# A cross-attention block followed by a recurrent block: head norm, softmax division and score issue rearranged, in a new order of work

## Chip, core and metric

One core of one Trainium2 chip runs the whole program. The metric is the device time of one execution in microseconds. Engines named here: PE is TensorE (PEld its weight loads), DVE is VectorE, ACT is ScalarE, POOL is GpSimd, SP is SyncE, whose queue issues nearly all DMAs.

## The reference

Eight batches, each of 128 channels by 256 positions, pass two layers. All of it is float32. Cut to what matters:

```
# layer 0: attention, 16 heads of 8 channels, 256 positions
q, kv = LN(x + pos), LN(ctx + pos)          # over the 128 channels
S = (q Wq)(kv Wk)^T / sqrt(8)               # per head, 256 x 256
y = softmax(S) (kv Wv);  r = y Wo + q
x1 = r + W2 gelu(W1 LN(r) + b1) + b2
# layer 1: recurrence, 128 tokens, 256 features = 32 heads of 8
xn = LN(x1); sx = shift(xn) - xn            # five mixes of xn and sx
r, k, v, gate, w = projections of the mixes
s_t = k_t v_t + w_t s_(t-1)                 # 8 x 8 state per head
out = r_t (u k_t v_t + s_(t-1))
att = head_norm(out) * gn_w + gn_b          # mean and variance over 8 features
x2 = x1 + (att * gate) Wo
out = x2 + sigmoid(xr Fr) * (relu(xk Fk)^2 Fv)
```

## The kernel before

**Stages.** A batch goes through four stages. Stage a (L373 to L399, and `top`): the two layer norms, projections q, k, v, and the split of q and k into three bf16 parts whose products give float32-like scores. The parts are written to DRAM (`spill`, L303) and read back stacked by head (`stack`, L309, 48 rows per head, even heads at partitions 0 to 47, odd heads at 64 to 111). `top` (PE L401, DVE L789) computes all scores with queries on partitions only to find each query's maximum; `guard` feeds the negated maxima back by DMA as two more rows. Stage h: `scores` again with keys on partitions (L422), `probs` as ACT exponentials (L609), `sums` (L437) as products with padded values whose extra columns of ones give the softmax denominators, `ctxn` the division, `wo`, a layer norm and the feed-forward (`h_centre` to `x1`). Stage r: layer norm, five mixes (`maa1` to `mixed`), projections `vg` and `rk` (16 instructions each), the decay, `values` and `v_rep` (values through DRAM and back, replicated), `kv` on POOL, two `scan` instructions on DVE. Stage o: `bonus`, `read`, head norm, gate, output projection, second layer norm, feed-forward and store.

**Order.** Nothing is scheduled at run time. The table `AT` gives every step an offset, `PERIOD` a distance between batches; `due` and `ticks` walk the sum, and each engine's instructions are issued in that order (L101 to L111). Only the order within an engine matters; waits are semaphores. In a full period the engines hold stage a of one batch, h of the batch ahead of it, r of the next ahead, and o of the one before that.

**Scores.** Heads alternate between two banks, `a_even` and `a_odd` (or `h_even`, `h_odd`). The PE issues head n once the consumer is through with head n-2, so it may write one bank while the other is read.

**Division.** `h_sum` has channels and denominators interleaved on partitions, queries along the free axis. DVE shuffles the denominators to the channels, takes a reciprocal of 128x256 elements and multiplies, twice (L801 to L810).

**Readout and head norm.** `read` uses the scanned state as weights and a 128x16 head indicator as the moving operand, 16 products per half, 32 instructions in a batch for both; the output has tokens on partitions. DVE adds the bonus, takes mean and variance over each head's 8 features in six steps (`heads`, L895), POOL the power -0.5 (`hrs`), DVE multiplies (`attn`), the PE turns it back (`turn_att`), ACT applies the affine (`ag`), DVE the gate (`agg`). `own` (PE L524, ACT L683) turns the values to tokens for this.

Of the kernel before, what the change touches and what calls it, by code (L numbers as in the profile page):

```python
# [9 lines left out]
ALU = mybir.AluOpType  # L10
ACT = mybir.ActivationFunctionType
AX = mybir.AxisListType
# [30 lines left out]
           ("FkT", 2 * E), ("FrT", 2 * E), ("FvT", 2 * E), ("heads", 16), ("Wo", 2 * C),  # L43
# [3 lines left out]
for _n, _w in WEIGHTS:  # L47
# [6 lines left out]
PERIOD = 729  # L54
# [3 lines left out]
        "load": 0, "spill": (1534, 1599, 1724), "stack": 1900, "guard": 1914, "values": 3359, "v_rep": (3409, 3436), "store": 4813,  # L58
    },
    "PE": {  # L60
        "centre": 1199, "var": 1234, "spread": 1293, "qk": 1350, "v": 1487,
        "top": (1627, 1638, 1663, 1672, 1690, 1705, 1739, 1740, 1762, 1811, 1825, 1834, 1846, 1864, 1878, 1887), "guard": 1919,
        "scores": (2108, 2123, 2265, 2278, 2311, 2338, 2341, 2350, 2399, 2405, 2428, 2495, 2549, 2561, 2587, 2598), "sums": (2354, 2370, 2571, 2623),
        "wo": 2731, "h_centre": 2743, "h_var": 2757, "h_spread": 2786, "ffn1": 2818, "ffn2": 2889, "turn1": 3075, "maa1": 3145, "maa2": 3191,
        "maa3": 3213, "vg": 3359, "rk": 3380, "decay1": 3393, "decay2": 3439, "own": 3465, "bonus": 3717, "read": (3745, 3790), "turn_att": 4018,
        "o_wo": 4061, "turn2": 4146, "ff_in": 4220, "ff_out": 4292,
    },
    "ACT": {
        "dev": 1125, "affine": 1312, "high": 1377, "v_pad": 1633, "middle": 1459, "guard": 1807,
        "probs": (2192, 2221, 2252, 2268, 2282, 2288, 2356, 2365, 2392, 2405, 2426, 2454, 2459, 2486, 2493, 2508), "h_dev": 2746, "fn": 2830,  # L70
        "to_gelu": 2761, "gelu": 2837, "to_exp": 3281, "xt1": 3115, "tanh1": 3137, "vt": 3245, "gate": 3359, "rk": 3300, "decay1": 3341,
        "decay2": 3385, "own": 3448, "ag": 3943, "xt2": 4068, "kk": 4265,
    },
    "POOL": {
        "zsum": 1074, "rstd_a": 1185, "rstd_h": 2861, "rstd1": 2978, "kv": (3413, 3666), "rst_low": 3695, "hrs": 3749, "rstd2": 3939,
    },
    "DVE": {
        "var_a": 1268, "nrm": 1285, "left": 1385, "parts": 1513,
        "top": (1621, 1621, 1667, 1675, 1696, 1708, 1787, 1791, 1812, 1825, 1837, 1870, 1887, 1909, 1914, 1928), "guard": 1931, "ctxn": (2702, 2718),
        "res": 2737, "var_h": 2754, "nrm_h": 2830, "x1": 3013, "norm1": 3053, "xh1": 3059, "sx1": 3094, "mix": (3179, 3283, 3337), "mixed": 3368,  # L80
        "ruk": 3456, "gate": 3903, "scan": (3484, 3632), "rst_high": 3739, "heads": 3802, "attn": 3917, "agg": 4072, "x2": 4152, "xh2": 4168,
        "xkr": 4193, "y": 4313, "yo": 4344,
# [31 lines left out]
def build(nc, x, ctx_in, weights, vecs, pos, first, out):  # L114
    with ExitStack() as stack:
# [60 lines left out]
        den = sb("den", [128, 2 * T])  # L176
        rden = sb("rden", [128, 2 * T])
        ctxn = sb("ctxn", [128, 2 * T])
# [22 lines left out]
        vt = sb("vt", [128, 2, NT])  # L201
# [845 lines left out]
```

## Time and profile before

| | us |
|---|---|
| median of 3 runs | 518.94 |
| lowest, highest | 516.72, 522.78 |
| the profiled execution's own time | 517.84 |
| its span | 516.0 |
| busy: PE, DVE, ACT, POOL | 399.4, 321.1, 209.1, 152.5 |
| mean granted PE clock | 0.851 of full |

Spans are the hardware profiler's. A row of a timeline gives start, duration, engine, line, operation, output and input, count, and in brackets the idle time before it and what ended it. Busy time of a pipelined PE is not PE at its peak.

### The profile page before, as it was taken

The numbers are of one execution on the slowest core, as the hardware profiler recorded it, in microseconds if no ns is written. First come the engines' busy times: TensorE is split into PE (matmuls) and PEld (weight loads), VectorE is DVE, ScalarE is ACT, GpSimd is POOL, SyncE is SP. The second block draws the span as 40 slices with busy tenths as digits, with TensorE's granted clock in tenths as the row PEclk, the third lists the DMA queues.
The fourth block names the chain that finished last, engine by engine and source line by source line (L and its number), as shares of the span: only waits on it lengthen the run. The fifth ranks groups of instructions, "written<-read, shape, count | busy, mean of one in ns | idle before, by whom it ended". The sixth has DMA issues, their size and how long they took to land.

```text
span 516.0 us, 6689 instructions
## 1 busy us (share of the span) xinstructions
PE 399.4 (77%) x2480; PEld 264.1 (51%) x2480; DVE 321.1 (62%) x674; ACT 209.1 (41%) x457; POOL 152.5 (30%) x102
## 2 busy tenths in 40 slices
PE   2436668879869998998899899989878988684624
PEld 1302322625656566557665674566556656573613
DVE  1134147247854896698769868967995583755611
ACT  1201423363454349246633744375446345115001
POOL 4100100110071227304540634172206406235240
PEclk9999999977966799699969978997998795778555
DMA  8430230050234024404230341035030012003000
GB/s 267 166 66 22 62 61 7 24 116 1 72 76 89 1 59 108 83 1 114 72 62 0 95 114 20 13 97 117 2 85 19 1 35 57 10 2 92 10 0 10
DMA packets 35952, 29.79 MB, mean 58 GB/s; under 512 B 3536, under 2 KB 33616, under 8 KB 35792
## 3 DMA queue, kind: packets, MB, share of 16 engines
q1 hardware_dynamic: 35776, 25.86, 21.1%
q10 hardware_dynamic: 144, 3.51, 1.7%
q8 instruction: 19, 0.31, 0.3%
q14 instruction: 13, 0.11, 0.1%
HBM read 20.85 MB, written 8.39 MB: 57 GB/s over the span
## 4 chain that ended last, share of the span: by engine, by line
PE 35%; DVE 22%; issue 14%; DMA 10%; POOL 8%; ACT 6%; SPq 5%; POOLq 0%; ACTq 0%; DVEq 0%
DVE top L792 8%; PE o_bank L540 5%; PE h_sum L445 5%; DMA v_rep<-values 5%; DMA k_stack<-stacks 4%; POOL v_rep L748 4%; DVE mixed L858 3%; PE r_one L355 3%; SPq L324 3%; PE a_even L411 3%; PE r_two L491 2%; PE o_bank L362 2%; DVE st L889 2%; PE h_even L472 2%; DVE mixed L867 2%
## 5 line engine op out<-in xcount | busy, mean ns | idle before, releaser
L792 DVE TENSOR_REDUCE top<-a_even 128x2 f32<-128x512 f32 x64 | 44.1, 689 | 41.5 <-PE a_odd L411 39.8
L616 ACT ACTIVATE probs<-h_even 128x512 f32<-128x512 f32 x64 | 38.1, 596 | 57.9 <-PE h_odd L433 40.2
L755 POOL TENSOR_TENSOR hrs<-hvar,mhalf 128x32 f32<-128x32 f32 x8 | 43.7, 5466 | 45.1 <-DVE hvar L915 45.1
L616 ACT ACTIVATE probs<-h_odd 128x512 f32<-128x512 f32 x64 | 38.5, 601 | 43.8 <-PE h_odd L433 23.1
L445 PE MATMUL h_sum<-probs,v_pad 128*32 128x256 f32 x512 | 49.3, 522 | 0.0
L411 PE MATMUL a_even<-k_stack,q_stack 48*128 48x256 bf16 x128 | 30.7, 329 | 23.0 <-DMA k_stack<-stacks 16.6
L734 POOL TENSOR_TENSOR rstd_a<-var_a,mhalf 128x4 f32<-128x4 f32 x8 | 8.3, 1041 | 125.9 <-DVE var_a L778 125.9
L792 DVE TENSOR_REDUCE top<-a_odd 128x2 f32<-128x512 f32 x64 | 43.7, 683 | 0.0
L540 PE MATMUL o_bank<-W,st 128*128 128x16 f32 x256 | 41.6, 308 | 2.4 <-DVE st L893 1.3
L540 PEld LDWEIGHTS o_bank<-W,st 128*128 128x128 f32 x256 | 40.1, 247 | 5.6 <-issue 2.3
L889 DVE TENSOR_TENSOR_SCAN st<-dec_rep,v_rep 128x1024 f32<-128x1024 f32 x16 | 39.0, 2440 | 5.2 <-POOL v_rep L748 5.0
L748 POOL TENSOR_TENSOR v_rep<-v_rep,rk 128x1016 f32<-128x1016 f32 x16 | 39.4, 2463 | 0.0
L433 PE MATMUL h_even<-q_stack,k_stack 50*128 50x256 bf16 x128 | 29.6, 319 | 5.1 <-ACT hid L632 2.8
L411 PEld LDWEIGHTS a_even<-k_stack,q_stack 48*128 48x128 bf16 x128 | 7.5, 99 | 50.1 <-DVE top L792 23.8
L411 PE MATMUL a_odd<-k_stack,q_stack 48*128 48x256 bf16 x128 | 30.9, 331 | 1.6 <-DVE top L792 1.6
L433 PE MATMUL h_odd<-q_stack,k_stack 50*128 50x256 bf16 x128 | 30.6, 327 | 1.3 <-ACT probs L616 0.3
L758 POOL TENSOR_TENSOR rstd_o<-var_o,mhalf 128x1 f32<-128x1 f32 x8 | 4.4, 552 | 91.7 <-DVE var_o L932 91.7
L807 DVE RECIPROCAL rden<-den 128x256 f32<-128x256 f32 x16 | 28.0, 1753 | 0.5
L445 PEld LDWEIGHTS h_sum<-probs,v_pad 128*32 128x32 f32 x512 | 16.9, 138 | 21.5 <-issue 18.3
L858 DVE SCALAR_TENSOR_TENSOR mixed<-r_one,vec,sx 128x128 f32<-128x128 f32 x48 | 13.8, 343 | 10.3 <-PE r_one L368 10.3
L377 PE MATMUL a_even<-zsum,W 128*128 128x512 f32 x16 | 11.7, 819 | 10.4 <-POOL zsum L731 9.3
L752 POOL TENSOR_TENSOR st<-st,rk 128x1024 f32<-128x1024 f32 x8 | 19.0, 2370 | 0.0
(155 smaller groups left out, 821.6 us busy)
## 6 DMA issues: line engine op xcount, KB each, us to landing
v_rep<-values SPq DMA_DIRECT2D x16, 511.5 KB, 6.1
W<-in_weights ACTq DMA_DIRECT2D x1, 3432.0 KB, 11.2
stacks<-parts SPq DMA_DIRECT2D x16, 192.0 KB, 2.2
q_stack<-stacks SPq DMA_DIRECT2D x16, 192.0 KB, 3.5
k_stack<-stacks SPq DMA_DIRECT2D x16, 192.0 KB, 4.5
stacks<-parts SPq DMA_DIRECT2D x16, 128.0 KB, 1.9
xin<-in_x SPq DMA_DIRECT2D x8, 128.0 KB, 4.5
xin<-in_ctx SPq DMA_DIRECT2D x8, 128.0 KB, 4.5
```

Of the source, the lines that this page charges most:

```text
L411: mm = pe.matmul(a_score[head % 2][:, j * T:(j + 1) * T], q_stack[g.p][e:e + SCORE_ROWS, head // 2, j * 128:(j + 1) * 128], k_stack[g.p][e ...
L433: mm = pe.matmul(h_score[head % 2][:, j * T:(j + 1) * T], k_stack[h.p][e:e + GUARD_ROWS, head // 2, j * 128:(j + 1) * 128], q_stack[h.p][e ...
L445: mm = pe.matmul(h_sum[quad * QUAD:(quad + 1) * QUAD, half * T:(half + 1) * T], v_pad[h.p][:, j, HEAD_ORDER[four * 4 + quad], :], probs[(f ...
L540: mm = pe.matmul(o_bank[:, (half * S1 + d) * 16:(half * S1 + d + 1) * 16], st[:, half, d, :], w("heads"), start=True, stop=True)
L616: act.activation(flat(probs[turn % PROBS][:, :, :]), h_score[HEAD_ORDER[turn] % 2][:, :], ACT.Exp, scale=SCORE_SCALE).then_inc(s_probs, 1)
L748: pool.tensor_tensor(kv[:, half, :, 1:NT], v_rep[:, half, :, 1:NT], rk[r.p][:, 1, half, None, 0:NT - 1].broadcast_to([128, S1, NT - 1]), A ...
L752: pool.tensor_tensor(st[:, 0, :, :], st[:, 0, :, :], rk[r.p][:, 0, 0, None, :].broadcast_to([128, S1, NT]), ALU.mult).then_inc(s_rst_low, 1)
L755: pool.tensor_tensor(hrs[:, :], hvar[:, :], mhalf[:, :], ALU.pow).then_inc(s_hrs, 1)
L792: dve.tensor_reduce(top[:, :, head], a_score[head % 2][:, :].rearrange("p (a t) -> p a t", a=2), AX.X, ALU.max).then_inc(s_top, 1)
L807: dve.reciprocal(rden[:, half * T:(half + 1) * T], den[:, half * T:(half + 1) * T]).then_inc(s_rden, 1)
L858: ins = dve.scalar_tensor_tensor(out=mixed[:, group, half, :], in0=src[:, col:col + 128], scalar=v(f"stack{group}_{half}"), in1=sx[:, half ...
L889: dve.tensor_tensor_scan(flat(st[:, half, :, :]), flat(dec_rep[r.p][:, half, :, :]), flat(kv[:, half, :, :]), 0.0, ALU.mult, ALU.add).then ...
```

## The change

Three computations are rewritten, and the table of offsets is replaced on all engines.

- **Pairs.** Two heads are issued together, even and odd alternating, for `top` and `scores`. The PE waits until both heads of the pair before have been consumed.
- **Division.** ACT copies `h_sum` to SBUF (`sums`), the PE transposes it (`turn_sums`, 4), DVE takes a reciprocal of 128x32 elements and multiplies 128x256 (`ctxq`), the PE transposes back (`turn_ctx`, 2), ACT copies (`ctxn`), and `wo` is one product in place of two.
- **Readout and head norm.** The state is the moving operand (128 columns), the weights are eight constant 128x128 matrices that also subtract the mean (`read`), and the bonus enters as a ninth product (`heads_centre`) in the same accumulation. Channels stay on partitions. ACT takes the weighted copy and the square (`att`), the PE sums the squares (`head_var`), POOL the power as before, ACT replicates it (`hrs_d`), the PE spreads it (`head_spread`), DVE multiplies, adds the bias and gates (`agg`). `own`, `turn_att`, `ag`, `heads`, `attn` go. `vt` is doubled.
- **Order.** All offsets are new. `ACT` runs `gate` ahead of `vt` and `to_exp` right behind `gelu`; DVE runs `var_a`, `scan0`, `nrm` in this order (before: `var_a`, `ruk`, `xkr`, `res`, `nrm`, `var_h`, `scan0`); `scan1` follows `parts`; on POOL `rstd_a` follows `kv1`. The weights grow by 1152 columns.

```diff
-PERIOD = 729
+PERIOD = 424
 AT = {
     "SP": {
-        "load": 0, "spill": (1534, 1599, 1724), "stack": 1900, "guard": 1914, "values": 3359, "v_rep": (3409, 3436), "store": 4813,
+        "load": 0, "spill": (849, 930, 1174), "stack": 1197, "guard": 1257, "values": 2052, "v_rep": (2069, 2077), "store": 3348,
     },
     "PE": {
+        "centre": 773, "var": 811, "spread": 815, "qk": 858, "v": 894, "top": (945, 972, 986, 1012, 1030, 1059, 1110, 1135), "guard": 1171,
+        "scores": (1243, 1283, 1296, 1344, 1383, 1399, 1434, 1445), "sums": (1319, 1431, 1442, 1504), "turn_sums": 1546, "turn_ctx": 1571,
+        "wo": 1592, "h_centre": 1596, "h_var": 1601, "h_spread": 1640, "ffn1": 1660, "ffn2": 1673, "turn1": 1774, "maa1": 1795, "maa2": 1822,
+        "maa3": 1856, "vg": 1900, "rk": 1979, "decay1": 2016, "decay2": 2024, "bonus": 2098, "read": (2142, 2207), "head_var": 2230,
+        "head_spread": 2321, "o_wo": 2375, "turn2": 2434, "ff_in": 2452, "ff_out": 2499,
     },
     "ACT": {
+        "dev": 780, "affine": 847, "high": 862, "v_pad": 904, "middle": 879, "guard": 1187,
+        "probs": (1276, 1282, 1302, 1308, 1319, 1329, 1358, 1366, 1385, 1389, 1393, 1393, 1412, 1419, 1457, 1459), "sums": 1542, "ctxn": 1580,
+        "h_dev": 1601, "fn": 1632, "to_gelu": 1677, "gelu": 1679, "to_exp": 1682, "xt1": 1782, "tanh1": 1807, "vt": 1949, "gate": 1893, "rk": 1995,
+        "decay1": 2015, "decay2": 2038, "att": 2215, "hrs_d": 2282, "xt2": 2437, "kk": 2474,
     },
     "POOL": {
+        "zsum": 597, "rstd_a": 834, "rstd_h": 1540, "rstd1": 1767, "kv": (1930, 2081), "rst_low": 2130, "hrs": 2197, "rstd2": 2292,
     },
     "DVE": {
+        "var_a": 834, "nrm": 849, "left": 860, "parts": 919,
+        "top": (964, 966, 978, 988, 1007, 1018, 1034, 1035, 1050, 1050, 1077, 1103, 1115, 1119, 1139, 1147), "guard": 1147, "ctxq": 1554,
+        "res": 1586, "var_h": 1591, "nrm_h": 1625, "x1": 1703, "norm1": 1704, "xh1": 1760, "sx1": 1804, "mix": (1847, 1854, 1880), "mixed": 1884,
+        "ruk": 2036, "gate": 2229, "scan": (2117, 2207), "rst_high": 2212, "bonus": 2125, "head_var": 2239, "agg": 2324, "x2": 2385, "xh2": 2401,
+        "xkr": 2437, "y": 2503, "yo": 2506,
     },
...
-                for head in range(H0):
-                    if g := due(at, "PE", "top", head):
...
-                        if head >= 2:
-                            pe.wait_ge(s_top, g.n * H0 + head - 1)
+                for pair in range(H0 // 2):
+                    if g := due(at, "PE", "top", pair):
...
+                        else:
+                            pe.wait_ge(s_top, g.n * H0 + 2 * pair)
                         for j in range(2):
+                            for e in range(2):
+                                rows = slice(64 * e, 64 * e + SCORE_ROWS)
+                                mm = pe.matmul(a_score[e][:, j * T:(j + 1) * T], q_stack[g.p][rows, pair, j * 128:(j + 1) * 128],
+                                               k_stack[g.p][rows, pair, :], start=True, stop=True)
                         mm.then_inc(s_scored, 1)
...
+                if h := due(at, "DVE", "ctxq"):
+                    groups = h_even[:, :].rearrange("p (g c) -> p g c", c=QUAD)
+                    dve.wait_ge(s_sums_T, h.n + 1)
+                    dve.reciprocal(rden[:, :, :], groups[:, :, DEN:QUAD:D0]).then_inc(s_rden, 1)
+                    dve.wait_ge(s_rden, h.n + 1)
+                    dve.tensor_tensor(ctxq[:, :, :, :], groups[:, :, 0:DEN].rearrange("p g (s d) -> p g s d", d=D0),
+                                      rden[:, :, :, None].broadcast_to([128, 16, 2, D0]), ALU.mult).then_inc(s_ctxq, 1)
...
                         pe.wait_ge((s_rst_low, s_rst_high)[half], o.n + 1)
+                        dst = o_bank[:, E + half * 128:E + (half + 1) * 128]
+                        pe.matmul(dst, w("heads_centre"), av[:, half, :], start=True, stop=False)
                         for d in range(S1):
-                            mm = pe.matmul(o_bank[:, (half * S1 + d) * 16:(half * S1 + d + 1) * 16], st[:, half, d, :], w("heads"),
-                                           start=True, stop=True)
+                            mm = pe.matmul(dst, w("read", d * 128, 128), st[:, half, d, :], start=False, stop=d == S1 - 1)
...
+                if o := due(at, "DVE", "agg"):
+                    dve.wait_ge(s_hspread1, o.n + 1)
+                    dve.wait_ge(s_attw, o.n + 1)
+                    dve.tensor_tensor(flat(attn[:, :, :]), o_bank[:, 0:E], flat(attw[:, :, :]), ALU.mult).then_inc(s_attn, 1)
```

## Rows read from the trace of the kernel before

**Rows 1.** The page: PE busy time, and the granted clock in 40 slices.
```profile
PE 399.4 (77%) x2480; PEld 264.1 (51%) x2480; DVE 321.1 (62%) x674; ACT 209.1 (41%) x457; POOL 152.5 (30%) x102
...
PEclk9999999977966799699969978997998795778555
```
**Rows 2.** Windows view; columns: stretch, length, busy us of PE, PEld, DVE, ACT, POOL.
```profile
248.07:295.56 47.49, 43.81 (x313) 30.25 (x312) 37.97 (x83) 24.94 (x55) 17.15 (x11) 0.89 0.26 62
295.56:344.90 49.34, 44.20 (x312) 30.24 (x311) 39.82 (x84) 26.60 (x60) 19.77 (x13) 0.90 0.24 60
...
295.56:312.60 17.04, 16.15 (x92) 11.24 (x90) 11.77 (x22) 10.03 (x23) 6.31 (x5) 0.74 0.41 101
264.80:292.98 28.18, 25.19 (x204) 16.58 (x202) 25.09 (x59) 13.23 (x31) 9.29 (x6) 0.97 0.18 44
```
**Rows 3.** Timeline of PE, the q projection of batches 2, 3 and 7.
```profile
99.43 1.06 PE L393 MATMUL a_even<-qn,W 128*128 128x256 f32 x2
...
148.72 1.06 PE L393 MATMUL a_even<-qn,W 128*128 128x256 f32 x2
...
344.90 0.60 PE L393 MATMUL a_even<-qn,W 128*128 128x256 f32 x2
```
**Rows 4.** Timeline, batch 0's maxima alone, first and second pair of heads.
```profile
33.59 0.69 DVE L792 TENSOR_REDUCE top<-a_even 128x2 f32<-128x512 f32 x1 [9.42 <-PE a_odd L411]
...
34.34 0.61 PE L411 MATMUL a_even<-k_stack,q_stack 48*128 48x256 bf16 x2 [0.78 <-DVE top L792]
...
34.99 0.69 DVE L792 TENSOR_REDUCE top<-a_even 128x2 f32<-128x512 f32 x1
```
**Rows 5.** Timeline, an even and an odd head's first score products.
```profile
268.91 0.28 PE L411 MATMUL a_even<-k_stack,q_stack 48*128 48x256 bf16 x1
...
268.93 0.28 PE L411 MATMUL a_odd<-k_stack,q_stack 48*128 48x256 bf16 x1
```
**Rows 6.** Groups by form: count, then busy us, mean ns, idle before.
```profile
L755 POOL TENSOR_TENSOR hrs<-hvar,mhalf 128x32 f32<-128x32 f32 x8 | 43.7, 5466 | 45.1 <-DVE hvar L915 45.1
...
L807 DVE RECIPROCAL rden<-den 128x256 f32<-128x256 f32 x16 | 28.0, 1753 | 0.5
...
L898 DVE TENSOR_TENSOR att<-vtok,o_bank 128x256 f32<-128x256 f32 x8 | 3.4, 420 | 14.1 <-PE o_bank L540 14.1
```
**Rows 7.** Timeline, a scan and the POOL powers that start near it.
```profile
244.69 2.28 DVE L889 TENSOR_TENSOR_SCAN st<-dec_rep,v_rep 128x1024 f32<-128x1024 f32 x1
...
244.85 2.62 POOL L737 TENSOR_TENSOR rstd_h<-var_h,mhalf 128x2 f32<-128x2 f32 x1 [0.21 <-DVE var_h L816]
...
293.84 0.71 POOL L737 TENSOR_TENSOR rstd_h<-var_h,mhalf 128x2 f32<-128x2 f32 x1
```
**Rows 8.** Timeline, from the last part to the first maximum product.
```profile
303.21 0.66 DVE L787 TENSOR_TENSOR parts<-left,parts 128x512 bf16<-128x512 f32 x1
...
312.60 0.10 PEld L411 LDWEIGHTS a_even<-k_stack,q_stack 48*128 48x128 bf16 x1 [0.81 <-DMA k_stack<-stacks]
```
**Rows 9.** Timeline of PE, blocks of float32 products at both clocks.
```profile
280.52 2.05 PE L355 MATMUL r_one<-mixed,W 128*128 128x128 f32 x16
...
451.40 2.22 PE L491 MATMUL r_two<-xx,W 128*128 128x128 f32 x8 [3.18 <-DVE xx L847]
...
479.84 7.01 PE L540 MATMUL o_bank<-W,st 128*128 128x16 f32 x32 [1.10 <-POOL st L752]
```
**Rows 10.** Timeline, passes of ACT and a chain through h_centre.
```profile
286.89 0.59 ACT L578 ACTIVATE dev<-a_even 128x512 f32<-128x512 f32 x1
...
289.92 1.99 ACT L681 ACTIVATE dec_rep<-dec 128x1016 f32<-128x1016 f32 x2
...
290.88 0.42 DVE L813 TENSOR_TENSOR res<-h_even,qn 128x256 f32<-128x256 f32 x1
...
293.59 0.15 DVE L816 TENSOR_SCALAR var_h<-h_sum 128x2 f32<-128x2 f32 x1
```
**Rows 11.** DMA issues: size of one, us to landing.
```profile
W<-in_weights ACTq DMA_DIRECT2D x1, 3432.0 KB, 11.2
```

More of the change, by code:

```diff
@@ L67 @@
     },
     "ACT": {
[L69 to L72, printed above, removed]
+        "dev": 780, "affine": 847, "high": 862, "v_pad": 904, "middle": 879, "guard": 1187,
@@ L76 @@
     },
     "DVE": {
[L78 to L81, printed above, removed]
@@ L420, in _ @@
                     mm.then_inc(s_guard_T, 1)
-                for turn in range(H0):
-                    if h := due(at, "PE", "scores", turn):
-                        head = HEAD_ORDER[turn]
-                        if turn == 0:
+                for pair in range(H0 // 2):
+                    if h := due(at, "PE", "scores", pair):
+                        if pair == 0:
                             pe.wait_ge(s_guard_in[h.p], dma(h, 4))
@@ L451, in _ @@
                         pe.wait_ge(s_weights, 16)
-                    pe.wait_ge(s_ctxn, nth(h, 2, 2))
-                    for half in range(2):
-                        mm = pe.matmul(h_even[:, 0:T], w("Wo", half * C, C), ctxn[:, half * T:(half + 1) * T], start=half == 0, stop=half == 1)
-                    mm.then_inc(s_wo, 1)
+                    pe.wait_ge(s_ctxn, h.n + 1)
+                    pe.matmul(h_even[:, 0:T], w("Wo"), ctxn[:, :], start=True, stop=True).then_inc(s_wo, 1)
                 if h := due(at, "PE", "h_centre"):
@@ L523, in _ @@
                     mm.then_inc(s_dec2, 1)
-                if r := due(at, "PE", "own"):
-                    pe.wait_ge(s_gate, r.n * 2 + 2)
-                    for half in range(2):
-                        mm = pe.transpose(r_one[:, half * 128:(half + 1) * 128], vt[:, half, :], ident)
-                    mm.then_inc(s_vtok, 1)
                 if o := due(at, "PE", "bonus"):
@@ L916, in _ @@
[L916 to L922 removed]
+                if o := due(at, "DVE", "bonus"):
+                    dve.wait_ge(s_bonus, o.n + 1)
+                    dve.tensor_tensor(flat(av[:, :, :]), o_bank[:, 0:E], flat(vt[o.p][:, :, :]), ALU.mult).then_inc(s_av, 1)
@@ new lines, in _ @@
+                if o := due(at, "DVE", "head_var"):
+                    dve.wait_ge(s_hvar1, o.n + 1)
+                    dve.tensor_scalar(hvar[:, :], o_bank[:, 0:H1], 1.0 / S1, EPS, ALU.mult, ALU.add).then_inc(s_hvareps1, 1)
+                if o := due(at, "DVE", "agg"):
+                    dve.wait_ge(s_hspread1, o.n + 1)
+                    dve.wait_ge(s_attw, o.n + 1)
+                    dve.tensor_tensor(flat(attn[:, :, :]), o_bank[:, 0:E], flat(attw[:, :, :]), ALU.mult).then_inc(s_attn, 1)
+                    dve.wait_ge(s_attn, o.n + 1)
+                    dve.wait_ge(s_gated, o.n + 1)
+                    for half in range(2):
+                        ins = dve.scalar_tensor_tensor(out=agg[:, half, :], in0=attn[:, half, :], scalar=v(f"gn_b_{half}"), in1=gate[o.p][:, half, :],
+                                                       op0=ALU.add, op1=ALU.mult)
+                    ins.then_inc(s_agg, 1)
@@ L995 @@
     put("heads", (np.arange(128)[:, None] // S1 == np.arange(16)[None, :]).astype(np.float32))
+    same = (np.arange(128)[:, None] // S1 == np.arange(128)[None, :] // S1).astype(np.float32)
+    put("same", same)
+    put("heads_centre", eye - same / S1)
+    put("read", np.concatenate([same * ((np.arange(128)[None, :] % S1 == d) - 1.0 / S1).astype(np.float32) for d in range(S1)], axis=1))
     for n in ("Wq", "Wk", "Wv"):
```

174 lines of the change are left out of this document (72 added, 102 removed).

## The prediction, as it was put on record

> **What bounds the kernel now.** I began with the page: the PE is busy 77% of the span, DVE 62%, and the clock line falls to five to seven tenths in places [rows 1]. That names no bound, since PE busy time is not PE at its peak. So I cut the trace at a step that comes once per batch, the q projection. Batches 3 to 7 are (344.90 - 148.72) / 4 = 49.0 us apart, batches 2 and 3 49.3 [rows 3]. In such a period DVE works 38 to 40 us, ACT 25 to 27, POOL 17 to 20 [rows 2]: no engine is full, and the loop is set by chains through engines that issue in order.
>
> Two stretches make the loop. From q projection to first maximum product takes 17.04 us [rows 2]: high part, left, middle, rest (`parts`), then the way through DRAM. `parts` starts at 303.21 and takes 0.66, the product starts at 312.60 as the DMA lands [rows 8]: 8.7 us that no reordering shortens. DVE works 11.77 of the 17.04, at clock 0.74. The other stretch, from first maximum product to the next `nrm`, is 28.18 long with DVE busy 25.09 [rows 2]: there DVE is the bound. One more thing counts: when a power on POOL starts just behind a DVE scan it takes 2.62 in place of 0.71 [rows 7]. The period without that meeting, 248.07 to 295.56, had 47.49; the one that follows, with it, 49.34 [rows 2].
>
> **The change part by part.**
>
> *Division.* It removes 2 x (1.75 + 0.42 + about 0.44 for the shuffle) = 5.2 us of DVE per batch [rows 6], the multiply priced as L898. It adds a multiply (0.42) and a reciprocal of 32 elements. No row has that; between nothing and 1.75/8 = 0.22 by size plus 0.15 of start [rows 6, 10], I take 0.33: 0.75 in all. On ACT it adds 0.6 and 0.4 [rows 10], on the PE six transposes for one product less, between 0 and 0.8, I take 0.3.
>
> *Head norm.* On DVE six passes and two multiplies, some 3.6 by the 0.42 of a pass [rows 6], become 1.6. DVE saves 5.2 + 3.6 - 0.75 - 1.6 = 6.4 us per batch. ACT gains a 0.4 square and two copies of half width and loses `own` and `ag`: net 1.4 with the division. POOL's 5.47 power stays [rows 6]; it ends before `head_spread` is reached on the PE.
>
> *Readout.* 32 instructions become 36 with 128 moving columns. At full clock a 128-column instruction is 2.05/16 = 0.13, at half clock 2.22/8 = 0.28; the old readout at half clock is 7.01/32 = 0.22 [rows 9]. So 36 x 0.28 - 7.01 = 3.0 more at half clock. In the full periods it ends before the stacked q and k land, so it costs nothing there; with that cover gone it would cost up to 3.0. In the tail one half may start before the other, so I take 2.1, bounds 0 to 3.0.
>
> *Pairs.* An even and an odd product already start 0.02 us apart when both are free [rows 5]. So pairing gives the PE nothing; what it does is lock PE and DVE in step. Batch 0 shows it bare: the next even product starts at 34.34, as soon as the even maximum is done, and its maximum at 34.99, so a pair takes 1.40 [rows 4]. Paired, the product waits for the odd maximum, 0.60 later. Seven gaps: 7 x 0.60 = 4.2 us. Batch 1 has it nearly as bare: 3.5, bounds 0 to 4.2. In full periods other DVE work partly fills the gaps; what it doesn't is in the walk below. The Trainium skill, page TensorEngine Tiling (Theoretical Speedup), gives up to 2x for a contraction of at most 64 rows. Taken as a gain of this change it would halve 64 products of 0.28, 9 us of PE busy time per batch; the trace has that overlap already.
>
> *Order.* I followed the new order by queue through one full period, with 0 at the first maximum product.
> - To the residual `res`, DVE has 25.09 - 5.2 (division) - 0.4 (`attn`) - 1.4 (`sx`, `xx`, `gate`, now earlier) - 2.3 (`var_a`, `ruk`, `xkr`, now later) + 1.5 (new work) = 17.3 us [rows 2, 6]. Waits come to 3.3: 0.7 in the first two pairs, behind `maa1` and `head_var` on the PE; 0.6 where the sixth pair is queued behind the 2.05 of `vg`; 0.7 for `o_wo`; the rest in transposes. `res` is done at 20.6.
> - Then DVE hardly matters. `res` to `var_h` takes 2.3 without `res` itself [rows 10], `ff_in` is queued behind `h_var` on the PE and takes 2.0 [rows 9], four of its twelve instructions being of double width: 24.3. ACT reaches `kk` only after `dec_rep` (1.99 [rows 10]), at 24.9, and is done with it at 26.0; `dev` takes 1.1 [rows 10], `var` and `var_a` 1.25: 28.35.
> - Now `rstd_a` and `scan0` start together. `var_a` then scan on DVE, with a power behind on POOL, is what `var_h` is today [rows 7]. It gives 1.05 alone, about 2.9 blocked: 29.4 or 31.2. `spread`, queued ahead of `ffn2` and `bonus`, takes 1.05, `nrm` 0.7 and `affine` 1.15: q projection at 32.8 or 34.5.
> - q projection to stacked q and k: 1.5, then four passes of 0.6 to 0.7 with handoffs, 2.8, then 8.7: 13.0. `scan1` now stands behind `parts`, which saves 4 of the 17.04.
>
> The Trainium skill, page SBUF — State Buffer (SBUF: two separate sides), says that a DVE operation with two SBUF inputs and a GpSimd one exclude each other for the whole instruction. The row agrees; by this rule it is 34.5.
>
> So a period is 34.5 + 13.0 = 47.5, or 45.8 unblocked, against 49.0. POOL's queue: `rst_low` and `rstd1` wait behind `rstd_a`, which delays `read`, still covered. SP's: `values` goes out earlier, `guard` behind both `v_rep`; by the walk its rows land some 4 us before `scores` wants them.
>
> *Weights.* 1152 columns are 576 KB more. At 3432 KB in 11.2 us [rows 11] that is 1.9 us of DMA, done by 20, before batch 0's parts leave; first needed near 90. Nothing; 1.9 if it collides.
>
> **The sum, against the profiled execution's 517.84.** +4.2 (batch 0) +3.5 (batch 1) -4.0 (the period from 99.43, which has no output stage: 49.3 against 45.3 by the same walk) -5 x 1.5 = -7.5 (five full periods) +2.1 (tail) = -1.7, so 516.1. That execution lies 1.1 under the median shown, so I say 517 us.
>
> **The rivals.**
>
> 1. *Forecast, lockstep and the blocked power eat the DVE saving (0.38):* 517, own range 511 to 523.
>
> 2. *The saved DVE time comes through (0.33).* For it: DVE is busy 25.09 of 28.18 in its stretch, and handoffs may overlap better than I walked. If `scan0` comes after `rstd_a`, the period is 45.8; with 1.3 less of waits, 44.5. Then 5 x 4.5 = 22.5 and 6 in the period before it: 517.84 + 7.7 + 2.1 - 28.5 = 499, 500 on the median's scale. Against it: ACT is full from 20 to 32 in the walk.
>
> 3. *Slower, by the PE's clock (0.29).* The PE is idle 2 us before `spread` and nearly 3 before the first maximum product, and sends less between. Today the granted clock in the stretch before that product averages 0.74 of 2.4 GHz, so part of it runs at 1.2, against 0.97 in the one behind it [rows 2]. If the fall also takes in `spread`, the q projection and the `maa1` and `head_var` ahead of the second pair, these grow by about 1.0, 1.0, 1.2 and 0.5, 0.28 an instruction against 0.13 [rows 9]: 3.7 per period, 51.2. From a period over 49.0 it decides. Then 5 x 2.2 = +11, 0 in the period before, +9.8: 538; with half of it (and half of the 4.0 kept) 531. I take 533, from the milder end, since the clock holds in today's denser stretch. The skill's page TensorE: Matmul & The Clock Gate (HAM oscillation) says idle gaps between bursts throw the clock back; by it alone I would be at this rival.
>
> **How the numbers follow.** A run can tell about 1% from no change, so faster means under 513.7, slower over 524.1. Case 2 lies in faster but for 0.03 of it; case 1 gives 0.08 to faster and 0.06 to slower; case 3 is over the line but for 0.01. Faster 0.38, same 0.28, slower 0.34. Predicted 517. For 8 in 10 the range takes in case 2's centre and case 3's: 494 to 535.
>
> **What would show it.** In the changed profile: batch 0's pairs 2.0 apart in place of 1.40; q projections of batches 3 to 7 47.5 apart; `rstd_a` at 2.6 or more in full periods, and `rstd_h` at 0.7; DVE busy 50 us less in all; q projection to first maximum product 13; readout some 0.13 an instruction with no wait behind it. The forecast fails if `rstd_a` stays at 1.05, if the PE waits for something other than the stack DMA at the first maximum, or if the mean clock falls below 0.8 (case 3).

## The result, and the profile after

The changed kernel takes 543.37 us (median of 4 runs, 542.92 to 544.57) against 520.86 us of the kernel before (4 runs, 516.72 to 525.12): a ratio of 1.046, 95% interval 1.038 to 1.054. The forecast was 517, 494 to 535: slower by 22.5 us, and outside the range. A ratio here and below is taken from undisturbed executions alone and a median from all of them, so the two can differ a little. The profiled execution took 543.78 us, its span is 542.0, against 516.0.

The page after, to be held against [rows 1]:

```profile
PE 386.0 (71%) x2560; PEld 271.3 (50%) x2560; DVE 285.2 (53%) x586; ACT 218.0 (40%) x481; POOL 148.6 (27%) x102
...
PEclk9999967669987978897888879787969999788766
```

DVE lost 35.9 us of work and the PE 13.4, and the span grew by 26. So no engine's load is the cause; it is what waits for what. The windows of two full periods, from q projection to q projection, with the columns of [rows 2], and the timeline of the q projections [rows 3]:

```profile
267.80:323.40 55.60, 46.06 (x321) 33.33 (x320) 35.19 (x72) 27.36 (x62) 18.72 (x11) 0.86 0.21 53
323.40:380.50 57.10, 47.26 (x322) 34.03 (x321) 35.53 (x72) 26.45 (x60) 18.71 (x11) 0.84 0.22 52
```
```profile
105.71 0.70 PE L391 MATMUL a_even<-qn,W 128*128 128x256 f32 x2 [0.73 <-ACT kvn L592]
...
154.45 0.59 PE L391 MATMUL a_even<-qn,W 128*128 128x256 f32 x2
...
380.49 0.59 PE L391 MATMUL a_even<-qn,W 128*128 128x256 f32 x2
```

Over these marks the difference splits as follows (before / after, us): to the second q projection 56.5 / 61.1, the next 42.9 / 44.6, the one from there 49.3 / 48.7, four full periods 196.2 / 226.1, the rest 171.1 / 161.5. That is +4.6, +1.7, -0.6, +29.9 and -9.6, in sum +26.0. The loss lies in the full periods: 56.5 us each, against 49.05 before and 47.5 in the walk.

Now the same timeline inside one period, at the three places where it leaves the walk. First the meetings of DVE and POOL:

```profile
303.12 2.33 POOL L760 TENSOR_TENSOR v_rep<-v_rep,rk 128x1016 f32<-128x1016 f32 x1
303.45 2.04 DVE L806 TENSOR_SCALAR guard<-top 128x32 bf16<-128x32 f32 x1
305.63 0.41 DVE L820 TENSOR_TENSOR res<-h_even,qn 128x256 f32<-128x256 f32 x1
...
315.03 2.29 DVE L896 TENSOR_TENSOR_SCAN st<-dec_rep,v_rep 128x1024 f32<-128x1024 f32 x1
315.17 2.96 POOL L746 TENSOR_TENSOR rstd_a<-var_a,mhalf 128x4 f32<-128x4 f32 x1 [3.38 <-DVE var_a L788]
318.18 2.08 PE L386 MATMUL a_odd<-W,rstd_a 128*128 128x128 f32 x8 [2.32 <-POOL rstd_a L746]
...
320.73 2.08 PE L483 MATMUL h_sum<-hid,W 128*128 128x256 f32 x4
322.60 1.06 PE L533 MATMUL o_bank<-ruk,W 128*128 128x256 f32 x2
```

The `kv` multiply on POOL runs from 303.12 to 305.45; the guard's first instruction, started 0.33 later, ends at 305.49, though it handles 32 elements. `res` stands behind it. `rstd_a`, started 0.14 after the scan, ends 0.81 after it: that one was foreseen. Whichever starts second is held until the first has ended. Behind `rstd_a` the PE has been idle 2.32 us, and `spread`, `ffn2` and `bonus`, all queued ahead of the q projection, run at half the rate of [rows 9]. It is so in most full periods, not in all: `spread` takes 2.06 to 2.08 in four of the five and 1.16 in one, behind the same 2.32.

The groups by form (mean in ns) show that this is not one period: the guard is held in four of eight batches, the shortest at 180 and the longest at 2350, where before all eight lay at 182; `rstd_a` is held in five.

```profile
L746 POOL TENSOR_TENSOR rstd_a<-var_a,mhalf 128x4 f32<-128x4 f32 x8 | 17.9, 2232 | 66.2 <-DVE var_a L788 66.2
L806 DVE TENSOR_SCALAR guard<-top 128x32 bf16<-128x32 f32 x8 | 9.6, 1197 | 0.3
```

Then the stretch behind the first maximum product, windows as above; the third number from the end is the granted clock as a share of 2.4 GHz:

```profile
280.30:285.00 4.70, 4.68 (x25) 3.19 (x26) 1.60 (x4) 0.97 (x4) 0.82 (x1) 0.52 0.00 0
285.00:290.00 5.00, 5.00 (x44) 4.06 (x44) 4.21 (x12) 1.62 (x4) 4.62 (x1) 0.76 0.01 2
290.00:305.00 15.00, 12.61 (x117) 8.11 (x115) 13.76 (x27) 5.96 (x14) 3.81 (x4) 1.00 0.33 89
...
320.00:325.00 5.00, 5.00 (x16) 3.33 (x14) 1.96 (x5) 2.05 (x4) 0.44 (x1) 0.51 0.02 3
```

For 4.7 us the PE is busy without a gap at the 1.2 GHz level, and DVE, with 1.60 of 4.70, waits for it. Ahead of it the PE had been idle:

```profile
280.32 0.28 PE L410 MATMUL a_even<-k_stack,q_stack 48*128 48x256 bf16 x1 [2.87 <-DMA k_stack<-stacks]
...
280.68 2.22 PE L497 MATMUL r_two<-xx,W 128*128 128x128 f32 x8
282.83 1.04 PE L549 MATMUL o_bank<-W,attsq 128*128 128x16 f32 x4
...
284.77 2.08 PE L366 MATMUL r_one<-th,W 128*128 128x128 f32 x8
286.64 1.40 PE L366 MATMUL r_two<-th,W 128*128 128x128 f32 x8
```

`maa1`, `head_var` and `maa2` stand on the PE between the first pair of heads and the third; the second pair's maximum waits for the PE 4 us in every such period.

### The profile page after: what moved, and what is told of

The parts are those of the page before. It is cut to its first block, busy times and chain, and to the rows that moved or that the text cites. A ratio compares the mean times of both kernels' runs of the same rounds, so it can differ in the third digit from the quotient of the medians.

```text
span 542.0 us, 6787 instructions
## 1 busy us (share of the span) xinstructions
PE 386.0 (71%) x2560; PEld 271.3 (50%) x2560; DVE 285.2 (53%) x586; ACT 218.0 (40%) x481; POOL 148.6 (27%) x102
## 4 chain that ended last, share of the span: by engine, by line
PE 40%; DVE 21%; issue 13%; DMA 9%; POOL 7%; ACT 5%; SPq 4%; POOLq 0%; ACTq 0%
DMA k_stack<-stacks 6%; DVE top L802 5%; PE o_bank L360 5%; PE r_one L353 3%; POOL rstd_a L746 3%; POOL hrs L767 3%; PE r_one L366 3%; PE o_bank L353 2%; PE r_two L497 2%; PE h_sum L442 2%; PE a_even L410 2%; DMA stacks<-parts 2%; PE a_odd L386 2%; PE h_sum L483 2%; SPq L305 2%
## 5 line engine op out<-in xcount | busy, mean ns | idle before, releaser
L410 PEld LDWEIGHTS a_even<-k_stack,q_stack 48*128 48x128 bf16 x128 | 9.7, 105 | 66.4 <-DMA k_stack<-stacks 38.9
L442 PE MATMUL h_sum<-probs,v_pad 128*32 128x256 f32 x512 | 37.5, 414 | 0.0
L760 POOL TENSOR_TENSOR v_rep<-v_rep,rk 128x1016 f32<-128x1016 f32 x16 | 37.4, 2339 | 0.0
L746 POOL TENSOR_TENSOR rstd_a<-var_a,mhalf 128x4 f32<-128x4 f32 x8 | 17.9, 2232 | 66.2 <-DVE var_a L788 66.2
L543 PE MATMUL o_bank<-st,W 128*128 128x128 f32 x256 | 34.2, 292 | 0.0
L543 PEld LDWEIGHTS o_bank<-st,W 128*128 128x128 f32 x256 | 33.0, 208 | 0.0
L386 PE MATMUL a_odd<-W,rstd_a 128*128 128x128 f32 x64 | 15.1, 411 | 14.4 <-POOL rstd_a L746 14.4
L386 PEld LDWEIGHTS a_odd<-W,rstd_a 128*128 128x128 f32 x64 | 13.2, 304 | 16.8 <-POOL rstd_a L746 16.6
L442 PEld LDWEIGHTS h_sum<-probs,v_pad 128*32 128x32 f32 x512 | 14.1, 116 | 14.2 <-issue 8.5
L749 POOL TENSOR_TENSOR rstd_h<-var_h,mhalf 128x2 f32<-128x2 f32 x8 | 5.9, 743 | 54.8 <-DVE var_h L823 54.8
## 6 DMA issues: line engine op xcount, KB each, us to landing
W<-in_weights ACTq DMA_DIRECT2D x1, 4008.0 KB, 12.7
```

The lines of the kernel that those rows point to most:

```text
L386: mm = pe.matmul(a_odd[:, j * 128:(j + 1) * 128], rstd_a[:, j:j + 1].broadcast_to([128, 128]), ident, start=True, stop=True)
L410: mm = pe.matmul(a_score[e][:, j * T:(j + 1) * T], q_stack[g.p][rows, pair, j * 128:(j + 1) * 128], k_stack[g.p][rows, pair, :], start=Tru ...
L442: mm = pe.matmul(h_sum[quad * QUAD:(quad + 1) * QUAD, half * T:(half + 1) * T], v_pad[h.p][:, j, HEAD_ORDER[four * 4 + quad], :], probs[(f ...
L543: mm = pe.matmul(dst, w("read", d * 128, 128), st[:, half, d, :], start=False, stop=d == S1 - 1)
L746: pool.tensor_tensor(rstd_a[:, :], var_a[:, :], mhalf[:, 0:4], ALU.pow).then_inc(s_rstd, 1)
L760: pool.tensor_tensor(kv[:, half, :, 1:NT], v_rep[:, half, :, 1:NT], rk[r.p][:, 1, half, None, 0:NT - 1].broadcast_to([128, S1, NT - 1]), A ...
```

## The experiments

Sixteen kernels, each timed beside the kernel before, whose median was 519.0 to 522.8 in the five groups, which ran on five chips. Differences between kernels of two groups carry this scatter of up to 3.8 us. Names of the parts: "meetings", a DVE and a POOL instruction of which the second is held; "single", heads one by one.

**1 to 4: parts of the change.** Both meetings moved apart:

```diff
-POOL "kv": (1930, ...   DVE "scan": (2117, ...
+POOL "kv": (1966, ...   DVE "scan": (2122, ...
```


> The changed kernel with two positions moved: `scan0` on DVE stands behind `nrm` instead of ahead of it, and the first `kv` multiply on POOL stands behind `rstd_h` instead of ahead of it. Nothing else differs. Theory M (the meetings of DVE and POOL set the loop): in each full period the guard's first instruction takes 0.2 us instead of 2.0 to 2.4, and `rstd_a` 1.05 instead of about 2.9; both stand on the chain from first maximum product to q projection, so a period shrinks from 56.5 by about 4, and five of them give 543 - 20 = 523 us. Theory C (the PE's clock and the queue ahead of the q projection set it): the two instructions get shorter, but the PE is then late with something else at half clock, and 535 us or more remain. If the moved multiply makes `rk`'s successors late instead (`rst_low`, `st`, `read`), DVE would show new waits before the readout, and the time stays at 543.

Measured 523.81 (522.51 to 527.67): -19.6. The guard's instruction is at 181 ns in all batches, `rstd_a` at 1013. It hit the number, in part by luck: from first maximum product to q projection full periods shrank by 5.7 to 6.7 us where 4 was expected, and from q projection to the next maximum product four of the five grew by 1.2 to 2.5 (why is told below, at `xt`). The move also brought something for nothing: the PE is idle 1.26 us ahead of `spread` in place of 2.32, and `spread`, `ffn2` and the q projection run at full clock:

```profile
304.56 1.16 PE L471 MATMUL a_odd<-W,rstd_a 128*128 128x128 f32 x8 [1.26 <-POOL rstd_a L831]
...
305.97 1.13 PE L568 MATMUL h_sum<-hid,W 128*128 128x256 f32 x4
...
307.63 0.70 PE L476 MATMUL a_even<-qn,W 128*128 128x256 f32 x2
```

Pairs undone, nothing else (scores and maxima with the loops and waits of the kernel before, each head at its pair's position):

```diff
-for pair in range(H0 // 2):    if g := due(at, "PE", "top", pair):
+for head in range(H0):         if g := due(at, "PE", "top", head):
```


> The changed kernel with heads issued one by one again (maxima and scores), each at the position of its pair. Theory L (lockstep costs only where DVE is bare): batch 0 gets back 4.6 us and batch 1 some 1.7, the full periods stay, 537 us. Rival: in full periods too each pair waits for the odd maximum, 7 x 0.6 = 4.2 us a period, which other DVE work does not fill: 543 - 6 - 5 x 4.2 = 516 us. If the pairs were a gain (both products off at once), it would be above 543.

Measured 534.24 (532.52 to 536.78): -9.1, between both. In the traces batch 0 gives 4.5, the second 0.7 and four full periods 4.6, while the rest of the span takes 2.2 back.

The new operations without pairs and in the old order, that is, the offsets of the kernel before with `turn_sums`, `turn_ctx`, `ctxn`, `att`, `hrs_d`, `head_var` and `head_spread` put in where their predecessors stood; and the same with pairs:

```diff
-PERIOD = 424   (all offsets new)
+PERIOD = 729   (offsets of before)
```


> The new division, head norm and readout in the order of the kernel before, heads issued one by one: the operations alone, without pairs and without the new order. Theory O (the loss is the order): the operations save 6.4 us of DVE per batch and put nothing on the chain, so the time is at or below that of the kernel before: 510 us, between 495 and 521. Theory N (the operations cost: more small products for the PE at half clock, and three more handoffs in the division): above 525, towards 543.

> As the kernel with the new operations in the old order, but with heads in pairs, each pair at the position of its odd head: everything of the change but the new order. Theory O: it stays well under 543; with lockstep in batches 0 and 1 (4.6 + 1.7) some 6 us above the same kernel without pairs, 516, and the rest up to 543 is the order. Rival L2 (lockstep costs in full periods too): 6 + 5 x 4 = 26 us above it, 536 or more, and the order costs little.

Measured 521.31 (516.97 to 524.09) and 536.43 (531.42 to 538.2). The kernel before had 520.81 on this chip. The first is at the upper edge of what was expected (510, 495 to 521): the operations gain nothing, though DVE works 273.5 us where it worked 321.1, and by the ratio of 1.017 (1.005 to 1.029) they may cost a little. The second is the rival's value, 536 or more, and not the theory's: pairs cost 15.1 there, 12.0 of it in four full periods. So by this way from the kernel before to the changed one the operations bring 0.5, pairs 15.1 and the new order 6.9; in the new order pairs are worth the 9.1 above. What pairs cost depends on what stands around them, and the loss is not the order's alone.

**5 to 8: the clock, and each meeting alone.** Three products on the PE ahead of the first maximum, whose result nobody reads, in the kernel with both moves:

```diff
 if pair == 0:
-    pe.wait_ge(s_stacked[g.p], dma(g, 4))
     pe.wait_ge(s_v_padded, g.n + 1)
     pe.wait_ge(s_left, g.n + 1)
+    for _ in range(3):
+        pe.matmul(a_odd[:, :], ident, W[:, 0:512], start=True, stop=True)
+    pe.wait_ge(s_stacked[g.p], dma(g, 4))
```


> The kernel with `scan0` and the first `kv` multiply moved (523.8 us), plus three products of 128x512 on the PE, whose result nobody reads, in the idle 3.5 us ahead of the first maximum product, after the wait for `left` and `v_pad` and before the wait for the stacked q and k. They take about 1.0 us each at full clock. Theory C (the PE's clock, fallen in that idle stretch, makes `maa1`, `head_var` and `maa2` behind it slow: 2.21, 1.04 and 3.58 us at 0.5 to 0.7 of full clock): with the PE kept busy they take 1.2, 0.7 and 2.0, DVE gets its second and third pair some 3.5 us earlier, and five to six periods give 523.8 - 19 = 505 us. Rival H (the stretch is set by handoffs and the order of queues, not by the clock): the products get shorter but the next wait takes over, 521 or more. If the added products end after the q and k have landed, each period is longer by what they overhang, up to 1 us.

Measured 509.59 (506.84 to 512.54): -14.2, ratio to the kernel before 0.983 (0.977 to 0.990). That is 14 of the 19 expected. With more work the PE is done sooner. Windows of the stretch behind the first maximum product, without and then with the three products:

```profile
270.70:275.10 4.40, 4.33 (x24) 2.95 (x24) 1.48 (x3) 0.66 (x3) 0.51 (x1) 0.55 0.00 0
275.10:280.00 4.90, 4.90 (x42) 3.90 (x40) 3.84 (x11) 1.93 (x4) 4.90 (x1) 0.71 0.00 2
```
```profile
262.60:267.00 4.40, 4.37 (x39) 3.58 (x40) 3.13 (x7) 1.51 (x4) 1.92 (x1) 1.00 0.00 0
267.00:272.00 5.00, 4.78 (x63) 2.23 (x61) 5.00 (x14) 2.75 (x6) 3.52 (x1) 1.00 0.03 7
```

Two such products ahead of `spread` in the changed kernel as it is, between the wait for `var_a` and that for `rstd_a`:

```diff
 if a := due(at, "PE", "spread"):
+    pe.wait_ge(s_vareps, a.n + 1)
+    for _ in range(2):
+        pe.matmul(a_odd[:, :], ident, W[:, 0:512], start=True, stop=True)
     pe.wait_ge(s_rstd, a.n + 1)
```


> The changed kernel as it is, with both meetings of DVE and POOL still in it, plus two such products of 128x512 on the PE between `var_a` and `rstd_a`, where the PE is idle 2.3 us. Theory C: `spread` takes 1.16 instead of 2.08, `ffn2` 1.1 for 2.1, `bonus` 0.6 for 1.06 and the q and k projections 1.3 for 2.0, all behind one another on the way to the q projection and the stacked q and k: 3 to 3.5 us less in each of five periods, 543 - 16 = 527. Theory M (only the blocked power itself counts): 541 to 543.

Measured 543.21 (535.83 to 544.53): a miss. `spread` fell to 1.16 and `ffn2` to 1.13, yet in the first three batches the added products, at half clock there, overhang: the fourth q projection starts at 157.9 in place of 154.4. The four periods from there take 221.2 in place of 226.1, 1.2 less each, a third of what was expected, and the mean granted clock is 0.816 in place of 0.853. The clock was lost in the early batches. Over the first two intervals between q projections it is 0.52 and 0.60, where the changed kernel has 1.00 and 0.73; in the four full periods it is 0.85 to 0.91, for 0.84 to 0.86. Why it is low there stays open; the kernel with the new operations in the old order has 0.59 and 0.65 there without any added product.

Each move alone:

> The changed kernel with only the first `kv` multiply on POOL moved behind `rstd_h`; `scan0` stays. The guard's first instruction falls from 2.0 to 2.4 us to 0.2, `res` and all behind it come 2.0 us earlier, and `rstd_a` stays at 2.9. Of the 19.6 us that both moves gave, this one should give 5 x 2.1 = 10: 533. If `rst_low` or `read` then comes late it gives less than 7.

> The changed kernel with only `scan0` on DVE moved behind `nrm`; the `kv` multiply stays. `rstd_a` falls from 2.9 to 1.05, 1.9 in each of six periods, and the PE is idle 1.3 us in place of 2.3 ahead of `spread`. Theory M: 543 - 10 = 533. Theory C in addition: at that shorter idle time the clock stays full over `spread`, `ffn2`, `bonus` and the projections, another 2 us or more each period, 525 or less, and most of the 19.6 us of both moves is this one's.

Measured 532.77 (529.02 to 534.41), -10.6, and 532.38 (527.74 to 533.53), -11.0. In the first the guard is at 181 ns and `rstd_a` at 2218; in the second 1213 and 1013. Both are at the expected 533, and they add up to 21.6, against 19.6 together. So each is a cause by itself, and about equal. With `scan0` moved alone `spread` takes 1.16 in all full periods, so the clock came along, but the 525 or less that was to follow from this did not come.

**9 to 11: why the saved DVE time was worth nothing.** Four maxima over a weight block, 2.5 us of DVE, whose result nobody reads, ahead of `var_a`, once in the kernel before and once in the one with the new operations in the old order:

```diff
 if a := due(at, "DVE", "var_a"):
+    for i in range(4):
+        dve.tensor_reduce(junk[:, i * 2:i * 2 + 2], W[:, 0:512].rearrange("p (a t) -> p a t", a=2), AX.X, ALU.max)
     dve.wait_ge(s_var, a.n + 1)
```


> The kernel before with 2.5 us more DVE work per batch, four maxima over a weight block whose result nobody reads, right ahead of `var_a`, where DVE has only 0.2 us of idle time. Theory E (two chains of equal length in that stretch, DVE's division and the PE's `centre`, `var`): DVE has no slack on this side, so it costs nearly its length in six periods, 520 + 6 x 2.2 = 533. Theory P (the PE alone set the stretch): under 524.

> The new operations in the old order, heads one by one (521.3 us), with the same 2.5 us of DVE work at the same place, where DVE now waits 3.7 us for the PE's `var`. Theory E: the idle time takes it in, and nothing changes, 519 to 524; so what the division saved on DVE was worth nothing there. If DVE still sets the stretch: 521 + 13 = 534.

Measured 544.2 (539.7 to 544.68), +25, and 526.06 (525.43 to 529.62), +4.7. With the division of before, 2.5 us more cost 5.6 in each of four full periods; with the new one, 0.2. Both medians are above what was expected, 533 and 519 to 524, the first by the new meeting named below; the second has a ratio of 1.015 (1.008 to 1.022), no more than the same kernel without the added work (1.017). The cleanest figure is the time from the guard to `var_a` in a full period: 7.08 before and 9.45 with the added work, 7.41 in both kernels with the new operations. Windows from the guard's first instruction to `nrm`, before and then with the new operations in the old order:

```profile
281.70:293.00 11.30, 9.76 (x64) 7.55 (x63) 9.34 (x26) 7.46 (x19) 4.45 (x5) 1.00 0.45 108
```
```profile
277.00:288.60 11.60, 9.55 (x66) 7.38 (x65) 5.11 (x19) 7.91 (x20) 5.15 (x5) 1.00 0.41 103
```

DVE does 4.2 us less and the stretch takes as long, because `var_a` now waits:

```profile
281.12 1.02 PE L460 MATMUL a_even<-zsum,W 128*128 128x512 f32 x2
...
283.33 1.05 PE L464 MATMUL a_odd<-W,devsq 128*128 128x1 f32 x8
...
284.42 0.16 DVE L874 TENSOR_SCALAR var_a<-a_odd 128x4 f32<-128x4 f32 x1 [3.75 <-PE a_odd L464]
```

Before, two chains of the same length ran beside each other here: DVE's reciprocals, and the PE's `rk`, `centre` and `var` with POOL and ACT between. They ended 0.3 us apart:

```profile
287.54 1.05 PE L381 MATMUL a_odd<-W,devsq 128*128 128x1 f32 x8 [0.23 <-ACT dev L578]
...
288.44 0.42 DVE L809 TENSOR_TENSOR ctxn<-h_sum,rden 128x256 f32<-128x256 f32 x1
...
288.78 0.15 DVE L778 TENSOR_SCALAR var_a<-a_odd 128x4 f32<-128x4 f32 x1
```

The excess over 2.5 in the first of the two kernels is a new meeting: its `xkr` began beside the `kv` multiply and took 3.21 for the 1.14 of before, the PE was idle 5.3 us behind it, and `h_centre` and `spread` ran at half clock.

Pairs alone, in the kernel before:

> The kernel before with heads in pairs alone (maxima and scores, each pair at the position of its odd head). Lockstep in the first two batches: 4.6 + 1.7 = +6.3. In full periods the kernel with the new operations lost 2 us a period by pairs where DVE was no bound; here DVE is fuller, so its work fills the gaps: +0 to +2 a period, 520 + 6 to 520 + 16, 531 by the middle. If pairs gain anything it is under 522.

Measured 531.17 (527.38 to 532.49): +11.9, as expected. In the traces batch 0 and the second cost 4.1 and 1.4, four full periods 5.0 and the rest of the span 2.9.

**12 to 16: putting it together.** The changed kernel with both moves and heads one by one, without and with the three products; then the scans moved in the two kernels with the old order (`scan0` behind `left`, `scan1` behind `parts`):

> The changed kernel with both meetings moved apart and heads one by one, without the added products that keep the PE busy. If the effects of the two moves (-19.6) and of single heads (-9.1) add: 543.4 - 28.7 = 515. Together with 503 us for the same kernel with the added products, the PE's clock is then worth 12 us here, as with pairs (14).

> The changed kernel with `scan0` and the first `kv` multiply moved, three products keeping the PE busy ahead of the first maximum product (509.6 us so far), and heads one by one again. If the effects add: batch 0 gives back 4.6, batch 1 1.7, full periods 0.5 to 1 each, 509.6 - 9 = 501, under both kernels. If pairs cost nothing once the clock stays up (odd and even products start together anyway, at 0.28 each): 503 to 505.

> The kernel before, with `scan0` on DVE moved behind `left` and `scan1` behind `parts`; nothing else. There `rstd_h` starts just behind `scan0` in most periods and takes 2.62 in place of 0.71, ahead of `h_spread` and the q projection. Theory M: it falls to 0.7, and four or five periods shrink by 1.5 to 1.9: 520 - 8 = 512. Rival: `st` comes later, the readout and the q and k in its place, and nothing is gained: 518 to 524.

> The new operations in the old order, heads one by one (521.3 us), with the same move of both scans. Here DVE has time to spare, so nothing is delayed by the move: `rstd_h` falls from 2.6 to 0.7 and a period from 49.5 to 47.8: 521 - 9 = 512. If it is under 505, DVE's saved time begins to count once the meeting is gone; if the idle time only moves to another wait, 519 or more.

Measured 516.09 (513.96 to 519.11); 502.95 (498.04 to 507.39), ratio 0.966 (0.957 to 0.975); 526.47 (523.83 to 530.51); 522.92 (520.23 to 525.61). The first is what adding the effects gives (515). The second lies between 501, if they add, and 503 to 505, if pairs cost nothing once the clock stays up, and does not tell these apart. In the last two the meeting went (`rstd_h` means 699 and 700 ns, from 1419 and 1915) and nothing was gained. The kernel before even became slower, by a ratio of 1.030 (1.011 to 1.049), past the 524 of the rival: from q projection to first maximum product it takes 18.2 to 19.6 in full periods, for 15.3 to 17.8. With the new operations the move made another meeting, on `yo`, with `bonus` waiting for it:

```profile
246.88 2.34 POOL L850 TENSOR_TENSOR st<-st,rk 128x1024 f32<-128x1024 f32 x1 [4.09 <-DVE st L982]
247.15 2.36 DVE L1034 SCALAR_TENSOR_TENSOR yo<-y,x 128x256 f32<-128x256 f32 x1
...
249.65 0.67 PE L619 MATMUL o_bank<-ruk,W 128*128 128x256 f32 x2 [2.15 <-DVE yo L1034]
```

The kernel with both meetings moved apart, and the 503 us kernel with it, has such a meeting too, made by the move of `scan0`: a copy of two columns, with `left` behind it.

```profile
308.72 2.34 POOL L849 TENSOR_TENSOR st<-st,rk 128x1024 f32<-128x1024 f32 x1 [4.22 <-DVE st L981]
...
309.73 1.36 DVE L924 COPY xt<-initial 128x2 f32<-128x2 f32 x1
...
311.28 0.68 DVE L879 TENSOR_TENSOR left<-a_even,parts 128x512 f32<-128x512 f32 x1
```
```diff
-DVE "left": 860
+DVE "left": 854   (ahead of x1)
```


> The 503 us kernel with `left` moved ahead of `x1` on DVE; nothing else. There a copy of two columns (`xt`) ahead of `left` takes 1.36 us in place of 0.15 beside POOL's first `st` multiply, so `left` comes 2.1 us after the high part is ready, and `parts`, the DMA and the first maximum product behind it. Theory M: `left` starts with the high part, `parts` comes 1.5 us earlier (it then waits itself for the end of that multiply), and six periods give 503 - 8 = 495. Rival: the added products ahead of the first maximum, or the readout before them, end later than the stacked q and k land, and the gain stops there: 499 to 503.

Measured 501.71 (497.72 to 503.45), ratio 0.965 (0.952 to 0.979). `left` starts with the high part, but `xh` (0.41, waiting for POOL's `rstd_r`) now stands ahead of `parts`, and a full period is 48.1. The expected 495 did not come; 499 to 503 was the rival. Against 503 that is within what the runs scatter. The two are the fastest versions, 3.4 to 3.5% under the kernel before by their ratios.

## Why the prediction was wrong, point by point

Stations of one full period in us from its first maximum product, beside the walk (its blocked value second; it names no time for `mixed`):

| | walk | changed | meetings apart | and PE kept busy |
|---|---|---|---|---|
| `mixed` done | | 13.3 | 13.4 | 10.5 |
| `res` done | 20.6 | 25.7 | 24.1 | 21.2 |
| `rstd_a` done | 29.4 / 31.2 | 37.8 | 33.7 | 30.9 |
| q projection | 32.8 / 34.5 | 43.1 | 36.9 | 34.0 |
| next product | 45.8 / 47.5 | 56.6 | 52.3 | 48.8 |

With the meetings apart and the clock up, the walk holds within 1.5 us of its unblocked value up to the q projection. The queue orders in it were right. (Its last terms, 1.05, 0.7 and 1.15, lead from 29.4 to 32.3 and not to 32.8; 3.1 was measured for them.) What it lacked was the state of two resources that no queue shows.

- **The failed step is "Order", from the first maximum product to `res` and on to the q projection.** It put `res` at 20.6, for 25.7 measured, with DVE's durations taken as they stood. By the table, 1.6 of these 5.1 us go with the meetings, 2.9 with the clock (the next point), and 0.6 stay. The guard's instruction was not walked against POOL, though the offsets show its new neighbour on POOL: the first `kv` multiply now ends its DMA wait just as the last maximum does. That is 2.0 us in four periods, and 10.6 in all by the run that removed it alone.
- **The products of that walk were priced at full clock.** Rival 3 had the right mechanism and named `maa1`, `head_var`, `spread` and the q projection; it was given 0.29 and a price of 3.7 a period. Keeping the PE busy ahead of the first maximum gave 14.2 us in all, where the span had grown by 26; `maa2`, which the rival did not name, took its part with 2.08 and 1.40. The rival named the nearly 3 us of idle time ahead of the first maximum; the reason against it, that the clock holds in today's denser stretch, set it aside, though the new order puts it right before products that others wait for. Before, the low clock lay mostly in the stretch ahead of the maximum (0.74, [rows 2]), and that this was work with slack was not tried. By the Trainium skill's page TensorE: Matmul & The Clock Gate (HAM oscillation) idle gaps between bursts throw the clock back; the traces agree with it in that stretch: with the meetings apart the clock is 0.55 behind 3.45 us of idle time, and 1.00 with the three products in the gap.
- **The blocked power was foreseen** (2.96 measured, 2.9 said), and its price was 1.7 a period; removing it gave 11.0 over five, 2.2 each, with the clock coming along. `rstd_h` fell to 743 ns, as said.
- **"DVE is the bound there" was half of the reading of [rows 2].** 25.09 of 28.18 busy is compatible with a second chain just as long, and the PE had 25.19 in the same row. Work added to DVE there cost its whole length (7.08 to 9.45), work taken away gained nothing (7.41). So the operations could not bring the -7.5: they alone are worth nothing (521.3 against 520.8). DVE's saving came out at 35.9 in all for the 50 forecast: 9.6 - 1.5 = 8.1 of the missing 14 is the held guard.
- **Batch 0: +4.2, measured +4.6.** Pairs 2.00 apart in place of 1.40, as said:

```profile
33.99 0.69 DVE L802 TENSOR_REDUCE top<-a_even 128x2 f32<-128x512 f32 x1 [9.75 <-PE a_odd L410]
...
35.99 0.69 DVE L802 TENSOR_REDUCE top<-a_even 128x2 f32<-128x512 f32 x1 [0.71 <-PE a_odd L410]
```

- **Batch 1: +3.5, measured +1.7.** In four full periods pairs cost 1.2 each in the new order, and 9.1 us in all; the forecast had them in the waits of the walk.
- **The period from the third q projection: -4.0, measured -0.6**. The period is 48.7; with `scan0` moved alone it is 44.8, with both moved 48.9, with the three products as well 45.8. So the blocked power and the clock both enter there; their shares stay open.
- **q projection to first maximum product: 13.0, measured 13.4.** In the kernels with `scan0` moved (and `left` not) it is 14.1 to 16.2 from the fifth batch on, because the move itself made the meeting on `xt`: from q projection to `parts` 5.0 with `scan0` moved alone, 3.2 with `kv` moved alone.
- **The rest, behind the last q projection: +0.6 (one full period of -1.5, and +2.1), measured -9.6.** The operations in the old order have 175.8 there for the 171.1 of before, so it is the order that shortens it; which part of it was not tried. The readout runs at 1.95 per half in full periods, 0.12 an instruction, with its cover in place.
- **Weights: no cost found.** 4008 KB landed in 12.7 us, and the first q projection starts at 19.4 in both.

Rival 2 fell: the power did come behind the scan, and DVE was not the only bound. The line drawn for failure, a mean clock under 0.8, did not catch it: the mean is 0.853, and was 0.851. The mean says nothing of who waits where it is low.

What could be got back in the new order, by the runs: both meetings 19.6 (the foreseen one alone 11.0), the clock ahead of the maxima 14.2, pairs 6.6 to 9.1. Together they lead from 543.4 to 503.0. That is more than the 26 us over the forecast, which had the foreseen meeting and a part of the pairs in it.

## What to carry to other kernels

Walk a new order not only queue by queue but against the neighbour engine: for each POOL instruction of 2 us, list the DVE instructions that may start beside it, and who stands behind them. A row in which one engine is busy nine tenths names a bound only if no other chain through the stretch is as long; add a little work to it before pricing what its removal gives. Look at the PE's idle time right ahead of products that others wait for, and fill it with products that nobody reads before any of them is moved; check in the early batches that they end before the wait does.

## What the runs showed of the hardware

- DVE instructions with next to nothing to do are held until a POOL multiply ends: 2.04 us for 32 elements to bf16 (0.18 alone), 1.36 for a copy of two columns (0.15). So are longer ones: 3.21 for the four of `xkr` (1.14), 2.36 for `yo` (0.42). The Trainium skill, page SBUF — State Buffer (Who interferes with whom), counts copies and `tensor_scalar` in their fast modes and operations with two SBUF inputs among those that exclude a GpSimd operation. The four rows agree in that all are held; whether the first two ran in such a mode no row shows. I had used the rule for the scan and the power alone.
- In these rows the one that starts second is held: the scan holds the power (2.96 in place of 1.0), the multiply holds the guard.
- The PE's clock was mostly at its lower level behind 2.32 us of idle time ahead of `spread` and at its upper one behind 1.26 us, in front of the same eight products (2.08 and 1.16 us). The idle time alone does not decide: once in the changed kernel they took 1.16 behind 2.32, and once, with the meetings apart, 2.08 behind 1.77.
- Three products that nobody reads, 2.74 us a batch at full clock, took 14.2 us off the kernel.
